# One kernel of attention and routed experts: the gate and address read from a deeper ring of landed tiles, a denser list of last steps, and one contraction moved ahead

## The reference, cut to what matters

```
x = layernorm(x + attention(x))                # causal, one head of 128, no parameters in the norm
logits = (x @ gate_w + gate_b) / 0.9           # 8 experts
keep the two largest, softmax over the two     # gate weights
f = sum over the two experts of gate * (gelu(x @ w1[e] + b1[e]) @ w2[e] + b2[e])   # 128 -> 512 -> 128
f = (f - mean) / sqrt(var + 1e-5) * ln_g + ln_b
x = layernorm(x + f)
```

## Time and profile before

| | us |
|---|---|
| median of 3 runs | 257.69 (257.65 to 258.29) |
| the profiled execution | 257.17 |
| its span, first to last instruction | 255.4 |
| TensorE busy in the span | 229.6 |
| ScalarE, VectorE, POOL busy | 179.3, 173.4, 144.3 |
| mean granted clock of TensorE | 0.97 |

### The profile page before, as it was taken

How to read it: one execution, slowest core, us unless ns; L and a number is a source line. 1 busy time by engine, 2 the same in 40 slices (tenths; PEclk the granted TensorE clock), 3 DMA queues, 4 the chain that set the end, 5 groups by cost and what they waited for, 6 DMA issues and landing times.

```text
span 255.4 us, 7300 instructions
## 1 busy us (share of the span) xinstructions
PE 229.6 (90%) x1874; PEld 209.0 (82%) x1875; DVE 173.4 (68%) x958; ACT 179.3 (70%) x527; POOL 144.3 (57%) x165
## 2 busy tenths in 40 slices
PE   6988998999999799999999999999999999999100
PEld 3466876788787689999999999999999999999100
DVE  0146576787888888558953333366488999989884
ACT  3365857778675889977886555555555996599953
POOL 8400007357777777777877777775544545546500
PEclk9999999999999999999999999999999999999855
DMA  5999303023131545523328797868789686913275
GB/s 143 250 332 332 105 3 93 31 74 97 53 95 53 137 134 120 144 68 107 95 75 254 204 355 241 221 183 246 228 267 356 186 232 180 320 47 114 92 220 151
DMA packets 45105, 42.38 MB, mean 166 GB/s; under 512 B 5488, under 2 KB 34080, under 8 KB 45072
## 3 DMA queue, kind: packets, MB, share of 16 engines
q1 hardware_dynamic: 40224, 32.84, 45.2%
q0 software_dynamic: 4320, 8.92, 10.0%
q10 hardware_dynamic: 528, 0.26, 0.3%
HBM read 27.89 MB, written 12.01 MB: 156 GB/s over the span
## 4 chain that ended last, share of the span: by engine, by line
PE 78%; DVE 10%; ACT 5%; DVEq 2%; issue 2%; DMA 1%; ACTq 0%; SPq 0%
PE bank L595 26%; PE bank L584 25%; PE bank L435 6%; PE bank L462 4%; PE bank L502 3%; PE bank L421 3%; PE bank L483 2%; ACT rows L668 2%; PE bank L450 2%; ACT probs L676 2%; PE bank L426 2%; PE bank L592 2%; PE bank L416 1%; DMA wk<-in_L_attn_W_K_dram 1%; DVE sum_stats L1139 1%
## 5 line engine op out<-in xcount | busy, mean ns | idle before, releaser
L749 ACT ACTIVATE h<-bank,b_cols 128x128 f32<-128x128 f32 x284 | 81.6, 385 | 37.4 <-PE bank L584 37.0
L1340 POOL DMA_INDIRECT returned<-x,slot_back x71 | 71.3, 1004 | 43.0 <-DVE x L1120 33.2
L1335 POOL DMA_INDIRECT slots<-rows,slot_of x64 | 65.0, 1016 | 53.0 <-DVE rows L984 34.4
L595 PE MATMUL bank<-w_all,h 128*128 x568 | 78.5, 282 | 0.0
L584 PE MATMUL bank<-slot_xT,w_now 128*128 128x128 f32 x568 | 75.2, 275 | 0.1
L595 PEld LDWEIGHTS bank<-w_all,h 128*128 128x128 f32 x568 | 69.0, 192 | 0.8
L584 PEld LDWEIGHTS bank<-slot_xT,w_now 128*128 128x128 f32 x568 | 69.1, 192 | 0.3 <-DVE slot_xT L883 0.3
L881 DVE CAST slot_back<-slot_x 128x1 uint32<-128x1 f32 x71 | 10.4, 147 | 37.9 <-PE bank L584 37.8
L838 DVE TENSOR_REDUCE negmax<-bank 128x1 f32<-128x128 f32 (+3 forms) x32 | 14.7, 484 | 16.0 <-PE bank L436 15.8
L462 PEld LDWEIGHTS bank<-v,probsT 128*128 128x128 f32 x160 | 19.7, 192 | 5.7 <-issue 3.8
L1120 DVE TENSOR_SCALAR x<-bank,slot_gate 128x128 f32<-128x128 f32 x71 | 24.0, 341 | 0.2 <-PE bank L595 0.2
(11 more groups left out here) (155 smaller groups left out, 305.4 us busy)
## 6 DMA issues: line engine op xcount, KB each, us to landing
w_now<-in_L_ffn_w_dram SPq DMA_DIRECT2D x47, 256.0 KB, 3.6
slot_x<-slots SPq DMA_DIRECT2D x71, 65.0 KB
w_all<-in_L_ffn_w_dram SPq DMA_DIRECT2D x16, 256.0 KB, 5.9
pair<-returned SPq DMA_DIRECT2D x14, 256.0 KB, 3.2
rows<-rows SPq DMA_DIRECT2D x8, 256.0 KB, 3.0
x<-n_L_attn_embeddings_dram SPq DMA_DIRECT2D x7, 256.0 KB, 3.9
returned<-x,slot_back POOLq DMA_INDIRECT x71, 3.4
slots<-rows,slot_of POOLq DMA_INDIRECT x64, 2.3
```

The source lines that it names most:

```text
L595: m = nc.tensor.matmul(o, h[:, s % RING, c * P:(c + 1) * P], w2_c, start=False, stop=(c == FC - 1))
L749: m = nc.scalar.activation(h[:, s % RING, cols], bank_[:, cols], ACT.Gelu, bias=b1_cols[:, c:][:, bass.ds(first, 1)])
L1335: g_.indirect_dma_start(slots, bass.IndirectOffsetOnAxis(ap=slot_of[:, b, c:c + 1], axis=0), rows[:, k, b * TB + t, :], None).then_inc(dis ...
L1340: g_.indirect_dma_start(returned, bass.IndirectOffsetOnAxis(ap=slot_back[:, j:j + 1], axis=0), y[:, j % Y_RING, :], None).then_inc(y_retur ...
```

## The change

- The ring of landed tiles `slot_x` is 24 deep and no longer 8. The copies of address and gate are gone: POOL reads the address and VectorE the gate in the landed tile. The address column is now written as an integer where it is made. SP loads tile j once tile j - 8 has been copied to `slot_xT` and tile j - 24 has been returned.
- TensorE's bodies 3 to 7 are written out.
- The pairs of batches 4 and 5 are both loaded at place 65 (before 69 and 70).
- The list of last steps takes 7 units a place from place 47, and batch 6's addition and first statistics (9 units) stand at its end, 157 in all. By the rule above the additions of batches 4, 5 and 6 fall in places 60, 62 and 68 (before 62, 63 and behind all), the first root of batches 4 and 5 in place 64 (before 66), and place 70 has no unit.
- The contraction of tile 67 stands ahead of the expansion of tile 70, the last one.

```diff
-        slot_x = sb("slot_x", [P, UNROLL, ROW])
-        slot_back = sb("slot_back", [P, J], U32)
-        slot_gate = sb("slot_gate", [P, 2 * UNROLL])
+        SLOT_RING = 3 * UNROLL
+        slot_x = sb("slot_x", [P, SLOT_RING, ROW])
...
-        LOAD_AT = {b: WHOLE[0] + 15 + b for b in range(4)} | {b: WHOLE[1] + 10 + b for b in (4, 5)}
+        LOAD_AT = {b: WHOLE[0] + 15 + b for b in range(4)} | {b: WHOLE[1] + 10 for b in (4, 5)}
...
-        FINAL_AT, FINAL_SHARE = WHOLE[0] + 7, 6
+        FINAL_AT, FINAL_SHARE = WHOLE[0] + 8, 7
...
-                    sp.wait_ge(slot_read, j - (UNROLL - 1))
+                    sp.wait_ge(slotT_ready, j - (UNROLL - 1))
                     sp.sem_inc(wait_held, 1)
+                    if j >= SLOT_RING:
+                        sp.wait_ge(y_returned[(j - SLOT_RING) % Y_RING], 16 * ((j - SLOT_RING) // Y_RING + 1))
...
+                    if last and s == LAST - 1:
+                        contract(J - LAG, (J - LAG) % UNROLL, e[s + 1]).then_inc(step_done, 1)
...
-            with pe.Fori(BOUND, BODIES - 1) as i:
+            for i in range(BOUND, BODIES - 1):
                 body(i, late=True)
...
-            for s in range(LAG):
+            for s in range(1, LAG):
                 contract(J - LAG + s, (J - LAG + s) % UNROLL, e[s]).then_inc(step_done, 1)
...
-                act.wait_ge(step_done, j + 1)
+                act.wait_ge(step_done, j + 1 + (1 if isinstance(j, int) and j == J - 1 else 0))
...
-                vec.tensor_copy(slot_back[:, bass.ds(j, 1)], slot_x[:, s % UNROLL, BACK:ROW])
-                vec.tensor_copy(slot_gate[:, j % (2 * UNROLL):j % (2 * UNROLL) + 1], slot_x[:, s % UNROLL, GATE:BACK]).then_inc(slot_read, 1)
                 vec.tensor_copy(slot_xT[:, s % RING, :], psT_of(j, s)).then_inc(slotT_ready, 1)
...
-                dve.wait_ge(step_done, i * UNROLL + (s + LAG + 1))
                 j = i * UNROLL + s
+                dve.wait_ge(step_done, j + LAG + (0 if j == J - LAG else 1))
...
-                vec.tensor_scalar(y[:, j % Y_RING, :], psY(s), slot_gate[:, j % (2 * UNROLL):j % (2 * UNROLL) + 1], None, ALU.mult).then_inc(y_ready, 1)
+                vec.tensor_scalar(y[:, j % Y_RING, :], psY(s), slot_x[:, j % SLOT_RING, GATE:BACK], None, ALU.mult).then_inc(y_ready, 1)
...
+            FINAL += [(what, 6, cost) for what, cost in HEAD]
...
-                add_pair(6)
-                take_moments(6)
                 finish_root(2)
...
-                g_.indirect_dma_start(returned, bass.IndirectOffsetOnAxis(ap=slot_back[:, j:j + 1], axis=0),
+                g_.indirect_dma_start(returned, bass.IndirectOffsetOnAxis(ap=slot_x[:, j % SLOT_RING, BACK:ROW].bitcast(U32), axis=0),
```

More of the change, by code:

```diff
@@ L219, in moe_block @@
         slot_loaded = [sem(f"slot_loaded{s}") for s in range(UNROLL)]
-        slot_read = sem("slot_read")
         wait_held = sem("wait_held")
@@ L304, in load_slots @@
             def load_slots(s, at):
-                sp.dma_start(slot_x[:, s, :], slots[bass.ds(at, P), :]).then_inc(slot_loaded[s], 16)
+                sp.dma_start(slot_x[:, s, :], slots[bass.ds(at, P), :]).then_inc(slot_loaded[s % UNROLL], 16)
             def load_pair(b):
@@ L369, in body @@
                         sp.wait_ge(emptied, 16)
-                    load_slots(s, at[s])
+                    load_slots(j % SLOT_RING, at[s])
                     if i == PADS_IN and s == tiles // 2 - 1:
@@ L501, in transpose_slots @@
                     pe.wait_ge(y_ready, i * UNROLL + (s - AHEAD - LAG - 3))
-                return nc.tensor.transpose(psT_of(i if not isinstance(i, int) else i * UNROLL + s, s), slot_x[:, s, 0:D], ident[:])
+                return nc.tensor.transpose(psT_of(i * UNROLL + s, s), slot_x[:, (i * UNROLL + s) % SLOT_RING, 0:D], ident[:])
             def step(b):
@@ L607, in body @@
                 tiles = LAST if last else UNROLL
-                e = expert_numbers(i * UNROLL, tiles)
+                e = expert_numbers(i * UNROLL, tiles + (1 if last else 0))
                 for s in range(FIRST_EXPANDED if first else 0, tiles):
@@ L1206, in final_unit @@
                     m = aggregate(b)
-                    if (b, again) in ((3, False), (5, False), (5, True)):
+                    if (b, again) in ((3, False), (5, False), (5, True), (6, False)):
                         m.then_inc(aggregated, 1)
@@ L1313, in _ @@
             for b in range(B):
-                g_.iota(rows[:, :, b * TB:(b + 1) * TB, BACK], [[N, TOPK], [1, TB]], base=b * S, channel_multiplier=TB,
+                g_.iota(rows[:].bitcast(I32)[:, :, b * TB:(b + 1) * TB, BACK], [[N, TOPK], [1, TB]], base=b * S, channel_multiplier=TB,
                         allow_small_or_imprecise_dtypes=True).then_inc(const_ready, 1)
@@ L1320, in _ @@
             pool.wait_ge(made, 4)
-            g_.iota(empty[:, :, BACK], [[P, BLOCKS]], base=TOPK * N, channel_multiplier=1,
+            g_.iota(empty[:].bitcast(I32)[:, :, BACK], [[P, BLOCKS]], base=TOPK * N, channel_multiplier=1,
                     allow_small_or_imprecise_dtypes=True).then_inc(const_ready, 1)
```

## The result

| | before | changed |
|---|---|---|
| median, us | 257.67 (257.56 to 259.42, 6 runs) | 264.99 (263.93 to 267.45, 6 runs) |
| ratio | | 1.0265, 95% interval 1.0226 to 1.0303 |
| profiled execution, us | 257.17 | 265.36 |
| its span, us | 255.4 | 263.5 |
| clock, mean | 0.970 | 0.968 |

Slower, as predicted, but by 7.3 us and not by 2.5, and outside the range. Runs of one kernel lie further apart than the opening says: by 3.2 us for the kernel before (256.96 to 260.16 in 29 runs, near 257.5 for the most part, and near 259.5), by 3.5 for the changed one, and by 4.4 in experiment 9.

What follows compares the result with a forecast made beforehand. TensorE's own work bounds the steps, VectorE having least room. Stop 2.2, ScalarE's later start 0.3, tail 0, copies 0: + 2.5 us, profiled 257.17 to 259.7, median 260.2 us predicted; range 258.7 to 261.8.

Steps and rivals of the forecast that it cites:

- Part 3: Pair loads at place 65: SP's wait there delays tile 66, so TensorE stops once, for 2.2 us.
- upper bound of 3.0: Longest stop of TensorE for tile 66, if tile 54's return is another 0.4 us late and the ramp is long.
- none of that moves to an earlier time: Tile 54's weighing and return, which end SP's wait, come no sooner; the pair loads are issued when they were before.
- Part 4: Seven units a place from place 47: VectorE needs 2.25 us a step, priced at nothing in the steps, at most 1 us.
- the rival with the clock: The clock falls in TensorE's stop, about 2 us more for one or two steps: 262 to 264 us, chance 0.04.
- the tail's new bound: VectorE stands 1 us longer at batch 6's addition, the last pair lands late: + 3.5 us, 261.2 us, chance 0.12.
- Part 5: One contraction ahead of the last expansion: ScalarE starts tile 70 2.5 us later, 0.3 us more than the stop.
- the tail's sum: VectorE's saved time becomes a wait for ScalarE's root, which comes 2.5 us later, at 243.3; the tail adds 0.
- The 2.0 us saved behind the last weighing: VectorE's time without batch 6's sum, statistics and moments in the tail, some 2.0 us, predicted to turn into a wait.
- the margin of 4.9 us: In the steps, how late VectorE's copy may be: made in step j, read in step j + 3.
- the parts priced at nothing: Copies removed, operands read from the landed tile, ring of 24, written-out loop: nothing, with 0.2 us either way for the loop.
- The ring's second wait: SP's added wait for the return of tile j - 24: may hold it about half a microsecond, priced at nothing.

Runs made afterwards that it cites:

- experiment 9: The changed kernel with both pair loads of batches 4 and 5 at place 66 in place of 65: 260.87 us, ratio 1.0119.
- experiment 1: The kernel before with one line changed, the pairs of batches 4 and 5 both loaded at place 65: 264.15 us, ratio 1.0243.
- experiments 9 and 10: The changed kernel with both pair loads at place 66 (260.87 us) and at place 67 (260.81 us, ratio 1.0134), in place of 65.
- experiment 3: The changed kernel with 28 small unused matmuls put between expansion 62 and transposition 66: 263.27 us, ratio 1.0214.
- experiment 8: The kernel before with the change's list alone (seven units from place 47, batch 6 in it): 263.07 us, ratio 1.0179.
- experiment 2: The changed kernel with the pair loads of batches 4 and 5 back at places 69 and 70: 261.67 us, ratio 1.0130.
- experiment 6: The changed kernel with pair loads at 69 and 70 and batch 6 added after the last weighing, seven units from 47 kept: 260.90 us, ratio 1.0119.
- experiment 5: The changed kernel with pair loads at 69 and 70 and the old list, batch 6 behind the last weighing: 259.43 us, ratio 1.0035.

## Why the prediction was right and wrong

**Right: the direction and its cause.** SP's long wait (8.3 us; 9.5 predicted), tile 66 behind it, one stop of TensorE released by that tile's DMA, and steps of 2.0 us again from the second one on. By the Trainium skill's advice to issue a DMA early and wait for it late ("DMA: Bandwidth & Descriptors", section "Rules for kernel authors") the loads at place 65 should have hidden their cost. Here they did not: their issue stood in SP's queue behind a wait of 8.3 us, and experiments 1, 9 and 10 show that this wait's place in the queue made the stop.

**The step that failed, first: the term "2.2 us" of Part 3.** The stop was 3.8 us. Taking 1.05 us off the times of after, to stand beside the prediction's:

| | predicted | measured | longer by |
|---|---|---|---|
| first pair load issued | 214.5 | 215.25 | 0.75 |
| tile 66 issued behind it | 1.9 later | 2.04 later | 0.14 |
| landing of tile 66 | 3.0 | 3.65 | 0.65 |
| stop | 2.2 | 3.8 | 1.6 |

The landing is the larger of the mis-sized terms, by experiment 1. There the list is that of before and the first pair load comes 0.1 us after the one of before; tile 66 takes 4.28 us to land, 1.3 more than predicted, and that alone makes the stop longer than its upper bound of 3.0 us. The prediction moved the four pair loads and the tile at 389 GB/s, as if nothing else moved; its 0.3 us for the completion no row shows. DMA from 217.3 to 222.0 us, changed kernel:

```profile
DMA packets 996, 1.54 MB, mean 328 GB/s; under 512 B 129, under 2 KB 325, under 8 KB 996
```

The four pair loads and tile 66 are 1.1 MB, so some 0.4 MB of other transfers went beside them, and the rate is 328. Of these 0.13 MB are in POOL's queue; the rest is in SP's, where it can only be the weights and tiles issued from 218.87 on.

The first pair load is 0.75 us late for two reasons. 0.36 is the choice of 214.5 where before has 214.86. The other is that "none of that moves to an earlier time" was only half of it: tile 54's return is issued at 213.67 - 1.05 = 212.62 against 211.49, 1.1 us later, behind a late VectorE; the return is then shorter than before and gives a part back. 0.4 us of the 1.1 is in the other traces with seven units a place too (211.9 in experiments 9 and 10, less their late starts); the rest goes with a wait of 0.78 us for an early batch's pair at 194 us, which those two do not have. Part 4 was priced as if it began at place 60, and place 58 holds the weighing on which everything in Part 3 hangs. In the changed kernel either term alone would have stayed just under 3.0 us.

**Second: the rival with the clock was the case, at a chance of 0.04.** Its threshold was drawn from the tail of before (2.9 us idle at 1.00), and the forecast of 2.2 us was put below it as if it were certain. The stop's own upper bound of 3.0 already touched it. It gave 1.8 us, shown by experiment 3, within the "about 2 us" that it was priced at. The section "HAM oscillation — how this bites in real kernels" of the Trainium skill's "TensorE: Matmul & The Clock Gate" tells of kernels that a wait for a DMA brings down to the lower clock, and the trace agrees: 0.83 in the ten microseconds from 220 us on, behind the stop.

**Third: the tail's new bound was the case too, at 0.12.** Batch 6's addition held VectorE 1.55 us, which held contraction 69 for 1.44 us and the last return until 250.07, and the last pair came 0.78 us after VectorE was ready for it. Less 1.05 us and the 3.4 us by which stop and clock went beyond the forecast, that return is issued at 245.6, against the 244.8 predicted. It cost 0.8 us; the prediction had given 1.0. Ahead of it the tail came as predicted but by another way: ScalarE's root was ready at 247.65, as in Part 5 and the tail's sum (ScalarE's row moved by the stop, the clock and 0.2 us), but VectorE asked for it only at 247.80 and never waited. The 2.0 us saved behind the last weighing were gone by 246.13, where that weighing waited for a contraction that had waited for VectorE. Both rivals came with the forecast and not in its place, and the text had added up only one at a time.

**Fourth: Part 4, "nothing in the steps, at most 1 us".** Under the stop this hardly shows: VectorE catches up while TensorE stands (it waits 1.2 us for an expansion then). The hold that Part 4 called its tightest came as worked out: VectorE waited 3.13 us for ScalarE's root, the copy of tile 68 ended at 233.73, and its expansion began at 234.88, a margin of 1.15 us where 1.2 was predicted. But alone the list costs 5.2 us (experiment 8), and 3.6 in the company of the other parts (experiment 2). The pace was right (2.25 us a place worked out; 2.16 on average from 206 to 217 us in experiment 6), but the prediction had the copy as the only thing that is late. The addition of batch 4 has no cover in place 60 with the loads at 69 (a wait of 2.3 us in experiment 2), and the contractions wait for VectorE's weighings, which the margin of 4.9 us says nothing of.

**Right, or nearly: the parts priced at nothing.** Copies, ring and address read there: POOL's return takes 1011 ns on average, within the 0.96 to 1.34 of before. The ring's second wait holds SP twice, at 120 to 150 us, for 1.4 us in all and 1.2 at the longest, where half a microsecond was predicted; TensorE waits for nothing from 100 to 200 us, so it cost nothing. The loop: ratio 1.0036 with 1 in its interval. Together with the contraction ahead, 1.0035 (experiment 5), 0.9 us by the ratio, not seen in the trace. That VectorE's saved time "gives 0.12 us a step if VectorE ever sets the pace" fits experiment 8 against 2 (1.4 us, though the contraction ahead also differs between them). And nothing was gained from batch 6's 2.0 us, as predicted.

**Not additive.** 6.1 us for the loads, 5.2 for the list, 7.3 for the change that has both. The stop gives VectorE the time that the list takes from it, and the missing copies take a part of the list's price away. That fits the sum, but how the 4.0 us of overlap divide between the two was not measured.

## What to carry to other kernels

A load moved forward in a queue that works in program order takes its semaphore wait with it: ask first when the wait ends, and then which load is behind it. Here the first place too early made TensorE wait 1.1 us, the second 3.6 and the clock fell with it, and no later place made it wait. Where a stop's length is a sum of four terms, take the upper bound with all of them late at once, compare that bound, and not the middle, with the idle time that the clock has been seen to bear, and let the rivals add up. An engine whose own pace is slower than that of the engine it serves (2.25 us against 2.0) has no free margin: it does not make good a wait that it meets. And look at the first microseconds of a profile before explaining the rest: a late start of up to 2.3 us stood in these traces beside effects of the same size.

## What the runs showed of the hardware

- The granted clock stayed at 1.00 during 3.6 us without a matmul and was 0.84, then 0.50, only after work had come back, until 226 us; 28 small bf16 matmuls in the same stop kept it at 1.00. It bore a wait of 1.1 us (experiment 9). The fall does not need work to come back: at the end of before the clock is 1.00 for 2.9 us without a matmul and falls in the microsecond behind, which has none either.
- The idle time of one wait does not decide it alone. With the loads at 67 TensorE had no matmul from 236.0 to 237.7 us, and the clock still fell, once it worked again:

```profile
236.00:237.00 1.00, 0.01 (x1) 0.00 (x0) 0.53 (x1) 0.98 (x3) 0.00 (x0) 1.00 0.33 88
237.00:238.00 1.00, 0.34 (x3) 0.32 (x4) 0.91 (x5) 0.99 (x2) 0.30 (x1) 1.00 0.02 4
238.00:239.00 1.00, 1.00 (x7) 1.00 (x7) 0.93 (x9) 1.00 (x4) 0.67 (x1) 0.62 0.00 0
```

- In traces of kernels whose programs for these instructions are the same, eight matmuls near 10 us took 1.13, 1.7 or 2.05 us.
- A load of 65 KB took 3.65 and 4.28 us from issue to landing behind four loads of 256 KB issued in the two microseconds before it.
